# A message-passing network's attention loop: gather indices copied two groups ahead, two small sets of transposes issued behind the next pair's query product

## The reference

```python
qkv = (node_embeddings @ W_qkv).reshape(nV, N, 3 * H)
q, k, v = jnp.split(qkv, 3, axis=-1)
scores = jnp.einsum('phi,phi->ph', q[src], k[dst]) / jnp.sqrt(jnp.float32(H))
m = jax.ops.segment_max(scores, src, num_segments=nV)
e = jnp.exp(scores - m[src])
denom = jax.ops.segment_sum(e, src, num_segments=nV)
w = e / denom[src]
wv = w[:, :, None] * v[dst]
att = jax.ops.segment_sum(wv, src, num_segments=nV).reshape(nV, N * H)
```

## Time and profile before

| | us |
|---|---|
| median of 3 runs | 7543.63 |
| lowest and highest of them | 7528.55, 7555.22 |
| the profiled execution, its time | 7550.91 |
| its span | 7549.1 |
| attention loop in it, first index copy to last addition | 5337.9 to 7062.7 |

### The profile page before, as it was taken

One profiled execution on the slowest core, in us unless ns is written; L12 is line 12 of the kernel. 1 busy time (PEld: TensorE's weight loads), 2 busy tenths in 40 slices (PEclk: granted clock), 3 DMA queues, 4 the chain that ended last, 5 costly groups with the idle time before them and its releaser, 6 DMA issues.

```text
span 7549.1 us, 118658 instructions
## 1 busy us (share of the span) xinstructions
PE 5261.9 (70%) x23723; PEld 3803.4 (50%) x23723; DVE 5513.5 (73%) x13389; ACT 2565.5 (34%) x9063; POOL 3753.8 (50%) x3981
## 2 busy tenths in 40 slices
PE   0277666772676666777467777799777777777798
PEld 0144444451444443333256666688555555555687
DVE  8887777538888775764489998511588888888666
ACT  0033333221333231111066666311455555555211
POOL 0177777414777773333367777300455555555111
PEclk9877777895777776888699999999898889898899
DMA  0133333213333432011345555455555555555311
GB/s 12 40 101 102 101 101 102 81 50 105 101 101 106 111 102 70 30 33 35 111 136 157 156 156 155 149 161 160 147 156 151 152 146 158 146 154 147 74 43 37
DMA packets 421993, 818.62 MB, mean 108 GB/s; under 512 B 75256, under 2 KB 268648, under 8 KB 420842
## 3 DMA queue, kind: packets, MB, share of 16 engines
q0 software_dynamic: 194048, 574.45, 27.6%
q1 hardware_dynamic: 225002, 231.00, 9.8%
q10 hardware_dynamic: 2304, 6.29, 0.3%
HBM read 688.72 MB, written 269.09 MB: 127 GB/s over the span
## 4 chain that ended last, share of the span: by engine, by line
PE 28%; DVE 23%; POOL 18%; issue 14%; DMA 11%; ACT 2%; POOLq 1%; DVEq 1%; SPq 1%; ACTq 1%
POOL ring L716 11%; PE ps L797 5%; PE ps L1415 5%; POOL big L1301 4%; DMA ring<-kv_d,gidx 4%; DVE big L1350 3%; PE ps L1843 2%; PE ps L1860 2%; PE ps L1617 2%; DVE big L338 2%; DVE big L339 2%; DMA ring<-x_d,idx 2%; DVE big L1747 2%; DMA big<-kv_d,gidx 1%; PE ps L1097 1%
## 5 line engine op out<-in xcount | busy, mean ns | idle before, releaser
L797 PE MATMUL ps<-ring 128*128 x3528 | 1498.4, 565 | 833.0 <-SPq L726 585.8
L797 PEld LDWEIGHTS ps<-ring 128*128 128x128 f32 x3528 | 742.0, 260 | 1271.3 <-issue 1215.5
L716 POOL DMA_INDIRECT ring<-in_x_dram,idx x832 | 834.4, 1003 | 578.7 <-DVEq L616 325.6
L778 ACT CAST ring<-ohb 128x128 f32<-128x128 bf16 x1764 | 523.5, 298 | 1691.2 <-DVE ohb L744 1646.7
L1537 POOL DMA_INDIRECT ring<-kv_d,gidx x754 | 713.2, 946 | 606.6 <-ACT gidx L1571 387.3
L1301 POOL DMA_INDIRECT big<-x_d,idx x832 | 798.6, 960 | 350.0 <-issue 213.5
L716 POOL DMA_INDIRECT ring<-x_d,idx x832 | 834.5, 1003 | 255.7 <-issue 235.8
L1365 PE MATMUL ps<-big,ring 128*128 128x128 f32 x4928 | 735.9, 294 | 298.0 <-DVE big L1340 155.3
L1365 PEld LDWEIGHTS ps<-big,ring 128*128 128x128 f32 x4928 | 629.3, 194 | 404.6 <-DVE big L1340 308.9
L754 DVE TENSOR_TENSOR big<-big,ps 128x257 f32 (+1 forms) x1764 | 754.2, 428 | 62.1 <-issue 29.7
L744 DVE TENSOR_SCALAR ohb<-iotab,keyf,nbase 128x128 bf16<-128x128 bf16 x1764 | 586.6, 333 | 234.7 <-PE ps L801 115.3
(11 more groups left out here) (370 smaller groups left out, 9536.8 us busy)
## 6 DMA issues: line engine op xcount, KB each, us to landing
bas_d<-big SPq DMA_DIRECT2D x1232, 128.0 KB
att_d<-wreg SPq DMA_DIRECT2D x464, 132.0 KB
big<-bas_d SPq DMA_DIRECT2D x49, 1024.0 KB, 5.6
x_d<-ring SPq DMA_DIRECT2D x147, 128.0 KB, 1.7
ring<-in_x_dram,idx POOLq DMA_INDIRECT x832
ring<-x_d,idx POOLq DMA_INDIRECT x832
big<-x_d,idx POOLq DMA_INDIRECT x832
kv_d<-ring SPq DMA_DIRECT2D x49, 260.0 KB, 2.3
```

The costliest lines, as they stand in the source:

```text
L716: nc.gpsimd.indirect_dma_start(out=rows[:, j, :], out_offset=None, in_=table, in_offset=bass.IndirectOffsetOnAxis(ap=idx_of(c), axis=0)).t ...
L778: S.copy(ohf[:, q % G1, :], ohb[:, q % G1, :]).then_inc(e["ohf"], 1)
L797: T.matmul(ps[k][:, 0:D], ohf[:, k, :], rows[:, slot, :].rearrange("p a d -> p (a d)"), start=True, stop=True)
```

## The change

Two edits, both in the attention loop.

1. **ACT.** The copying of a group's indices moves into a function `indices(c)`, and step c copies those of the group at c + 8 (`AHEAD = 2 * GRP`); at c = 0 the groups 0 and 4 are copied as well. The registers that say which edge column a chunk takes are kept in `of_group` for the keys, which are still formed at step c. The wait for the earlier gather of the same index slots goes along with the copy; the wait for `b3["gk"]` stays with the keys.
2. **PE.** The transposes of the ends move from the end of step 2 to step 4, behind that step's query product (pair 2) and ahead of L1643. Those of the carries move from the end of step 4 to step 6, behind the query product of pair 4. What they wait for is unchanged, and no instruction is added or taken away.

```diff
--- before.py
+++ after.py
@@ -1543,6 +1543,19 @@
             S = nc.scalar
             act.wait_ge(tabs_back, 16 * 5)
             act.wait_ge(b3["init"], 1)
+            of_group = {}
+            AHEAD = 2 * GRP
+
+            def indices(c):
+                g, i = c % R3 // GRP, c // R3
+                if i:
+                    got, base = got3[g]
+                    act.wait_ge(got, base + 64 * i)
+                of = load_group(mybir.EngineType.Activation, chunk_i, c, GRP, NCK - 1)
+                for a in range(GRP):
+                    last = S.copy(gidx[:, g, a:a + 1], idx[:, bass.ds(of[a], 1)])
+                last.then_inc(got_idx, 1)
+                of_group[c] = of
 
             def step(c, j, i):
                 if j % 2:
@@ -1561,15 +1574,14 @@
                     S.activation(oh3[:, jj:jj + 2, :].rearrange("p s n -> p (s n)"), far[:, t, :], ACT.Relu,
                                  bias=ones[:, 0:1], scale=-1.0).then_inc(b3["oh"], 1)
                 if j % GRP == 0 and live(c, 0, N3):
-                    g = j // GRP
+                    if c == 0:
+                        for cc in range(0, AHEAD, GRP):
+                            indices(cc)
+                    if c + AHEAD < N3:
+                        indices(c + AHEAD)
+                    of = of_group.pop(c)
                     if past(c, R3):
-                        got, base = got3[g]
-                        act.wait_ge(got, base + 64 * i)
                         act.wait_ge(b3["gk"], NT + (c - R3) // B3 + 1)
-                    of = load_group(mybir.EngineType.Activation, chunk_i, c, GRP, NCK - 1)
-                    for a in range(GRP):
-                        last = S.copy(gidx[:, g, a:a + 1], idx[:, bass.ds(of[a], 1)])
-                    last.then_inc(got_idx, 1)
                     for a in range(GRP):
                         last = S.activation(pk[:, j + a:j + a + 1], keyf[:, bass.ds(of[a], 1)], ACT.Identity,
                                             bias=nbase[:, bass.ds(c + a, 1)], scale=1.0)
@@ -1617,6 +1629,17 @@
                         last = T.matmul(ps[t][:, a * D:(a + 1) * D], ohT[:, t, a * P:(a + 1) * P],
                                         QN[:, bass.ds(at[(j - 2) % GRP + a], 1), :].rearrange("p a d -> p (a d)"), start=True, stop=True)
                     last.then_inc(l3["q"], 1)
+                if j % B3 == 4 and batch_at(c, j, i, 4) is not None:
+                    pe.wait_ge(b3["ends"], NT + batch_at(c, j, i, 4) + 1)
+                    for k, end in enumerate((fwd[:, P - 1:P], keysT[:, P - 1:P], bwd[:, 0:1], keysT[:, 0:1])):
+                        last = T.transpose(ps[6][0:1, k * P:(k + 1) * P].rearrange("a (m n) -> a n m", m=HEADS), end, ident[:, :])
+                    last.then_inc(b3["rows"], 1)
+                if j % B3 == 6 and batch_at(c, j, i, 6) is not None:
+                    pe.wait_ge(b3["car"], NT + batch_at(c, j, i, 6) + 1)
+                    pe.sem_inc(s_fill, 1)
+                    for k in range(2):
+                        last = T.transpose(ps[6][:, k:k + 1], car[:, k, :], ident[0:1, 0:1])
+                    last.then_inc(b3["col"], 1)
                 if j % B3 == 8 and batch_at(c, j, i, 8) is not None:
                     b = batch_at(c, j, i, 8)
                     hot = oh3[0:1, (j - 8 - B3) % R3, :]
@@ -1642,17 +1665,6 @@
                     for a in range(2):
                         last = T.matmul(ps[3 + t][:, 0:AV], oh3[:, jj + a, :], weighted[:, t, a * AV:(a + 1) * AV], start=(a == 0), stop=(a == 1))
                     last.then_inc(l3["pv"], 1)
-                if j % B3 == 2 and batch_at(c, j, i, 2) is not None:
-                    pe.wait_ge(b3["ends"], NT + batch_at(c, j, i, 2) + 1)
-                    for k, end in enumerate((fwd[:, P - 1:P], keysT[:, P - 1:P], bwd[:, 0:1], keysT[:, 0:1])):
-                        last = T.transpose(ps[6][0:1, k * P:(k + 1) * P].rearrange("a (m n) -> a n m", m=HEADS), end, ident[:, :])
-                    last.then_inc(b3["rows"], 1)
-                if j % B3 == 4 and batch_at(c, j, i, 4) is not None:
-                    pe.wait_ge(b3["car"], NT + batch_at(c, j, i, 4) + 1)
-                    pe.sem_inc(s_fill, 1)
-                    for k in range(2):
-                        last = T.transpose(ps[6][:, k:k + 1], car[:, k, :], ident[0:1, 0:1])
-                    last.then_inc(b3["col"], 1)
             walk(pe, N3, R3, LAG_PV, step, flat=True)
 
         def l3_edges_dve(dve, q):
```

## The result

| | before | after |
|---|---|---|
| median, us | 7539.78 (4 runs) | 7466.89 (4 runs) |
| lowest to highest | 7528.55 to 7555.22 | 7457.15 to 7484.07 |
| profiled execution, its span | 7550.91, 7549.1 | 7457.15, 7455.3 |

The changed kernel takes 0.990 of the time of the kernel before (95% interval 0.9881 to 0.9919): 73 us less, where 127 were forecast. That is 1.0% and clear of the noise; it lies inside the range, with 0.57 of the gain that was forecast.

What follows compares the result with a forecast made beforehand. DVE was taken to bound the attention loop; 1.37 (edit 2) + 0.72 + 0.1 (edit 1) = 2.19 us a batch, times 58 = 127 us, from 7543.6 to 7417 us; range 7370 to 7475.

Steps and rivals of the forecast that it cites:

- the rival in which the gather waits stay: Attention loop: slots, not indices, decide, or gathers land later; only edit 2's 80 us are gained, 7464 us; chance 0.16.
- The bound and its waits: Attention loop: DVE is the bound, 87% busy, waiting 1.37 us a batch for PE and 1.33 for gathers.
- Edit 2, the old waits: DVE's product waits for PE's query product at pairs 2 and 4 go: 1.37 us a batch, 80 us over 58.
- and none takes its place: With the ends moved, DVE reads their row only at about 6040.1, after they are ready at 6039.56: no new wait.
- behind the waiting carries now stands only the sum of step 6: PE's stream: the moved carries delay only that sum, which DVE's own weighting L1763 holds back anyway.
- PE's clock comes back late: Rival: thinner PE work behind the carries raises the clock later; two more cold steps a batch give 7605 us; chance 0.07.
- the waits only change their name: Rival: DVE's addition L1735 waits for PE's step 8 sum behind the transposed weights; time within 0.3% of before; chance 0.06.
- Edit 1, the indices: POOL's gathers for pair 12 start 0.86 us earlier; gain 0.72 us a batch there, 0.1 at the next pair 0.
- The reading that slots, not indices, set pair 0: Gathers need ring slots (32) freed by DVE's weighting L1763; pair 0's group was still forecast to gain 0.1 us a batch.
- the first rival: All waits go: POOL starts or gathers land sooner, DVE waits for nothing; 157 us less, 7387 us; chance 0.13.
- what would show it: Profile signs: query wait under 10 us, gather waits about 25 to 35, clock near 0.89; wrong if sum wait exceeds 20.
- POOL's releaser: Sign in the profile after: POOL's first gathers name DVE's weighting L1763 as releaser, no longer the index copy.

Runs made afterwards that it cites:

- the fastest run: Changed kernel, clamped, with unused identity transposes in three PE stands: 22 ahead of the carries' wait, 6 behind the carries, 14 ahead of the transposed weights; 7421.86 us, ratio 0.9845.
- one group ahead: Changed kernel, clamped, with the indices copied one group ahead instead of two (AHEAD = GRP); 8511.40 us, ratio 0.995 to the kernel before in its session.
- the first four experiments: Changed kernel with the clamp alone, 7471.48 us; with it, only the indices edit, 7483.72; only the transposes edit, 7492.22; carries back at step 4, 7478.81.

## Why the prediction was right in sign and too large in size

The time lies in the range, but partly by luck. The slow end of the range was set for the rival in which the gather waits stay (7464), and 7467 came about otherwise: the gather waits shrank, and new waits for PE, which the sum had at nothing, took nearly as much as edit 2 freed.

- **The bound and its waits: right.** DVE was the bound, and what the change moved were its waits. Counts stayed and busy times nearly, as the earlier trace rows and the page after show, and what the loop lost in period is the whole gain.
- **Edit 2, the old waits: right.** Both waits for the query product, at pairs 2 and 4, went from 75.5 us to none.
- **Edit 2, "and none takes its place" and "behind the waiting carries now stands only the sum of step 6": this step failed.** The sum of 1.37 us a batch had no term for what a thinner run behind the carries does to the clock. Measured: 46.4 us at the addition of pair 6 and 19.1 at the product of pair 8, together 65.5 us or 1.19 a batch, nearly all of it in the 23 late batches. The mechanism stood in the text as the rival "PE's clock comes back late", and its place was right (the short steps of DVE later in the batch), but I gave it the choice of deciding the sign or nothing. It came in part: in 23 of 55 batches, at 2.74 - 0.16 = 2.58 us, 59 us in all, against a shortfall of 127 - 73 = 54 us. From the earlier trace rows I could have read that the clock came back just ahead of the weights, 6 us behind the carries, so with no margin, and given it a term of its own. What edit 2 is worth depends on what else is there: 0.85 us a batch alone, 0.12 to 0.19 with the indices ahead, in place of 1.37.
- **The rival "the waits only change their name"** had the right instruction, L1735's successor waiting for PE's sum, for the wrong reason. In the batches with the clock back in time it waits for 0.16 us on average.
- **Edit 1, the indices: right in mechanism, near in size.** The start moved from 1.69 to 0.80 us behind the weighting, by 0.89 where 0.86 was taken. The gather waits fell by 73.0 - 34.5 = 38.5 us or 0.70 a batch, of 0.82 forecast. The split was off: pair 12 lost 49.9 us (39.6 forecast), and pair 0 grew by 9.5 where it should have lost some. The reading that slots, not indices, set pair 0 was in the text and was not priced. That edit 1 alone gives 1.14 us a batch, with fewer waits for the query product too, was not foreseen.
- **The case for the first rival**, the Trainium skill's advice to issue a DMA early ("DMA: Bandwidth & Descriptors", Rules for kernel authors), was worth half: 34.5 us of gather waits stay in the change and 38.6 in the fastest run, and 166 of 176 first gathers in the change start 0.80 us after a weighting, so it is the slots that hold them.
- **Of what would show it**: gather waits of 25 to 35 (34.5) and the query wait at its old places (0) came; the clock near 0.89 came (0.88); a new wait for PE's sum over 20 us, named as a sign of a wrong forecast, came too, and is what cut it. POOL's releaser wasn't named by the view; the constant 0.80 us stands in its place.
- **0.25 us a batch are not in the waits named.** The addition had 7.3 us of waits before too, so the new ones are 65.5 - 7.3 = 58.2 us or 1.06 a batch; 1.37 + 0.70 - 1.06 = 1.01 by the waits named, and 1.26 measured. Of the rest, 0.18 is DVE's busy time, which fell from 25.27 to 25.09 us a batch with the same instructions (its product took 0.688 us on average and takes 0.681), and 0.07 is in hand-overs too short to be listed. Why its instructions got shorter no run tells.

Open besides: whether one group ahead suffices, which of the three fillings is needed where the kernel before takes 7540 us, why the clock falls at one moment in one batch and at another in the next, and what more slots would do for the 35 us of gather waits.

## What to carry to other kernels

Moving work out from behind a wait can take it from where it brought TensorE's clock back: before counting the freed wait as gain, look in the windows at when the clock comes back and which short step comes right after, and give that step a price for the share of iterations in which it will be cold. Average clock and total busy time don't show this; splitting the iterations by the length of one fixed instruction (1.16 or 1.97 to 2.13 us here) does. And try each edit alone and on top of the other: here the second was worth 0.85 us a batch by itself and almost nothing beside the first. If stands are filled with idle work, look where the idle time goes: one filled stand passed it on to the next.

## What the runs showed of the hardware

- **With three stands filled the clock stayed at 1.00.** In the change the stands of 3.0, 0.8 and up to 1.0 us behind each other in a batch went with a mean of 0.88; with these three filled it did not fall in any regular batch, though PE still stood for 1.3 us ahead of the transposes of the scores. The rule that a low clock is the resting state and that activity lifts it (the Trainium skill, "TensorE: Matmul & The Clock Gate", What's actually happening) agrees with both in direction.
- **The same loop goes two ways.** With no difference in the work, the clock was back for the sum behind the weights in 32 batches (by 6.3 us behind the carries) and not in 23 (from 9.8 us on), as the table above has it by the moment of its fall.
- **Unused transposes are cheap.** 22 transposes of the identity took 2.56 us, 0.12 us each, in a stand that is idle anyway.
- **The same program was 13 to 15% slower in some sessions.** The kernel before took 8546.59 us (16 runs) and 8662.18 us (14 runs) there, against 7540. It need not be the chip: the record numbers the chip of the 8547 us and that of the first four experiments both as 2. In these traces DVE waits for releasers that the trace does not hold ("remote"), as in this row of its waits in the run with one group ahead:

```profile
DVE wreg L1748 <- remote: 81.1, 36, 3.7
```

In the traces of the other sessions there is none. PE is late at one place there besides: in that run DVE waits for it for 81.5 us around pair 10 (49.6 at the product, 31.9 at the addition), in each of the other kernels of these sessions for 43 to 112, and elsewhere for nothing. Of the 1044 us by which that run exceeds the change's 7467, only 58 x (31.63 - 27.98) = 212 are in the attention loop. What causes it no run here tells. It left the times of seven runs without an answer to what they were made for, and only waits and batches within one trace could still be read.
